# Layer norm, attention with rotary positions and a SwiGLU in one kernel: moments of two batches shared by tiles between two engines, two chunks of gate and up moved ahead, jobs reordered, first scores set between the last units of the prologue

## The reference

```python
xn = layernorm(x)                                  # no affine part
q, k, v = xn @ Wq.T + bq, xn @ Wk.T + bk, xn @ Wv.T + bv   # q: 16 heads of 8; k, v: 4 heads of 8
q, k = q * cos + rotate_half(q) * sin, k * cos + rotate_half(k) * sin
p = softmax(q k^T / sqrt(8))                       # over 1024 keys, per batch and head
attn = (p @ v) @ Wo.T + bo
ffn = (silu(xn @ wg.T) * (xn @ wu.T)) @ wd.T       # 384 hidden; int32 weights times 1/127
out = x + attn + ffn
```

## Time and profile before

| | |
|---|---|
| median of 3 runs | 758.31 us (757.91 to 759.13) |
| profiled execution | 758.32 us |
| span in the trace (first to last instruction) | 755.8 us |
| mean granted TensorE clock | 0.995 of full |
| busy: PE, DVE, ACT, POOL | 722.8, 683.1, 624.0, 228.7 us |
| first row maximum on DVE | 28.25 us |
| end of the prologue's weigh(0, 0, 0) | 65.82 us |

### The profile page before, as it was taken

One profiled execution on the slowest core, in us unless ns is written; L12 is line 12 of the kernel. 1 busy time (PEld: TensorE's weight loads), 2 busy tenths in 40 slices (PEclk: granted clock), 3 DMA queues, 4 the chain that ended last, 5 costly groups with the idle time before them and its releaser, 6 DMA issues.

```text
span 755.8 us, 13786 instructions
## 1 busy us (share of the span) xinstructions
PE 722.8 (96%) x4933; PEld 218.8 (29%) x4934; DVE 683.1 (90%) x1262; ACT 624.0 (83%) x1303; POOL 228.7 (30%) x373
## 2 busy tenths in 40 slices
PE   6899999999999999999999999999999999999987
PEld 5532222232222222232322222232322222232322
DVE  5898999999999999999999999999999999999931
ACT  4536988888898988889888888889888888989886
POOL 3676762235412762112021211211121221202100
PEclk9999999999999999999999999999999999999999
DMA  9334331011311112011111101011110101110020
GB/s 297 102 130 115 109 115 43 1 40 26 116 33 34 33 65 84 2 32 33 33 33 33 33 2 45 21 33 34 33 33 27 39 2 33 33 33 2 2 85 29
DMA packets 30723, 38.26 MB, mean 51 GB/s; under 512 B 5600, under 2 KB 20448, under 8 KB 30400
## 3 DMA queue, kind: packets, MB, share of 16 engines
q1 hardware_dynamic: 27680, 30.18, 14.0%
q0 software_dynamic: 1440, 4.72, 1.7%
q10 hardware_dynamic: 1536, 2.49, 1.0%
HBM read 23.28 MB, written 11.53 MB: 46 GB/s over the span
## 4 chain that ended last, share of the span: by engine, by line
PE 75%; DVE 14%; ACT 6%; DMA 2%; issue 2%; SPq 0%; POOL 0%; ACTq 0%; DVEq 0%; POOLq 0%
PE acc_ps L1184 29%; PE banks L1080 20%; DVE mx L925 13%; PE banks L1100 10%; PE banks L1104 7%; ACT probs L719 5%; PE banks L1191 4%; PE banks L1199 3%; DMA y_all<-in_x 2%; PE banks L1162 1%; PE banks L1040 1%; PE banks L1234 1%; PE banks L1207 1%; PE banks L1061 0%; DVE row_max L931 0%
## 5 line engine op out<-in xcount | busy, mean ns | idle before, releaser
L925 DVE TENSOR_REDUCE mx<-banks 128x1 f32<-128x512 f32 x1024 | 638.4, 682 | 30.0 <-PE banks L1080 26.7
L719 ACT ACTIVATE probs<-banks 128x512 f32<-128x512 f32 x1024 | 549.2, 606 | 93.3 <-PE banks L1100 88.1
L1100 PE MATMUL banks<-qc,kc 51*128 51x512 bf16 x1024 | 304.9, 383 | 11.2 <-ACT probs L719 6.1
L1080 PE MATMUL banks<-ka,qa 48*128 48x512 bf16 x1024 | 301.8, 382 | 7.4 <-DVE mx L925 7.4
L1184 PE MATMUL acc_ps<-probs,v_grp 128*32 128x512 f32 x2048 | 273.4, 606 | 1.2 <-ACT probs L719 1.0
L1080 PEld LDWEIGHTS banks<-ka,qa 48*128 48x128 bf16 x1024 | 67.1, 94 | 291.3 <-DVE mx L925 246.2
L578 POOL TENSOR_TENSOR neg_max<-row_max,nought 128x16 bf16<-128x16 f32 x32 | 7.1, 222 | 316.8 <-DVE row_max L931 309.5
L1100 PEld LDWEIGHTS banks<-qc,kc 51*128 51x128 bf16 x1024 | 64.3, 94 | 45.7 <-ACT probs L719 42.5
L1104 PE MATMUL banks<-xn_T,w_ffn 128*128 128x256 f32 x192 | 66.3, 429 | 0.0
L1184 PEld LDWEIGHTS acc_ps<-probs,v_grp 128*32 128x32 f32 x2048 | 40.3, 108 | 85.7 <-ACT probs L719 58.8
L602 POOL TENSOR_TENSOR gated<-gu 128x256 f32<-128x256 f32 x48 | 35.3, 735 | 73.7 <-ACT gu L801 73.7
(11 more groups left out here) (108 smaller groups left out, 354.5 us busy)
## 6 DMA issues: line engine op xcount, KB each, us to landing
qa<-q_rows SPq DMA_DIRECT2D x28, 192.0 KB, 3.4
qc<-q_rows SPq DMA_DIRECT2D x56, 96.0 KB, 2.7
q_rows<-part POOLq DMA_DIRECT2D x18, 256.0 KB, 4.1
ka<-k_later SPq DMA_DIRECT2D x24, 96.0 KB, 2.1
kc<-k_later SPq DMA_DIRECT2D x24, 96.0 KB, 2.2
out<-y_all SPq DMA_DIRECT2D x16, 128.0 KB, 2.0
y_all<-in_x SPq DMA_DIRECT2D x3, 512.0 KB, 11.9
k_rows<-part SPq DMA_DIRECT2D x6, 256.0 KB, 3.0
```

Source lines behind the costliest of these rows:

```text
L719: nc.scalar.activation(probs[:, s % SLOTS, j, :], banks[:, score_bank(g, G * s + j), :], ACT.Exp, scale=SCALE).then_inc(exp_done, 1)
L925: nc.vector.tensor_reduce(out=mx[:, h, col, k:k + 1], in_=ps, op=ALU.max, axis=AX.X).then_inc(max_done, 1)
L1080: nc.tensor.matmul(ps, qa[par][rows, j // 2, t * P:(t + 1) * P], ka[par][rows, k * W:(k + 1) * W], start=True, stop=True).then_inc(a_ready, 1)
L1100: nc.tensor.matmul(banks[:, score_bank(g, u), :], kc[par][rows, kt * P:(kt + 1) * P], qc[par][rows, h, j // 2, :], start=True, stop=True). ...
```

## The change

- **Moments.** ACT now makes sums and squares of tiles 0 to 3 (HT = 4) of batches 1 and 2; DVE takes tiles 4 to 7 of batches 1 and 2 and all of batch 3. DVE does its four tiles of batch 1 ahead of the first rotation, the others later. An epsilon step for ACT's sums (add_eps_sums) comes beside the one for DVE's tiles. The squares of batch 2 stand between the splits on ACT.
- **Low part.** Both halves' third parts are subtracted by DVE (low); POOL's subtraction goes.
- **FFN.** Parts 0 and 1 of group 0's gate and up are multiplied between the replications (after the third part of half 0, and after the first of half 1); part 2 follows unit 6. They use banks 0, acc_ps and 1, so the transposes of batch 1 use banks 2 and 3. keep_busy is left only ahead of half 0's replications.
- **Order of the jobs.** The query projection of batch 1 comes at units 8 and 10, values at 20 and 22, the last head at 24 to 30, the values' transposes at 32 and 34, queries of batches 2 and 3 at 36 to 42. ACT's copies and the numbers waited for follow (RAW_Q, RAW_LAST). The first maxima are transposed behind unit 37, not 36.
- **First scores.** The four scores of step 0 are issued behind units 44, 45, 46 and 47.

```diff
-PE_XN, PE_FFN, PE_S1, PE_V = (2, 4, 10, 12, 14, 16), (5, 7, 9), (18, 20, 22, 24), (26, 28)
-PE_VT, PE_Q = (33, 35), (30, 32, 37, 39, 41, 43)
-IDLE_X, IDLE_PARTS = 20, (3, 3, 0, 4, 2, 4)
-NEG_BEHIND = HU + 4
+PE_XN, PE_FFN, PE_Q1, PE_V = (2, 4, 12, 14, 16, 18), 6, (8, 10), (20, 22)
+PE_S1, PE_VT, PE_Q = (24, 26, 28, 30), (32, 34), (36, 38, 40, 42)
+IDLE_X, IDLE_PARTS = 20, (3, 3, 0)
...
-        xnt_banks = (banks[:, 0, :], acc_ps[:, :])
+        def xnt_bank(b, h):
+            return banks[:, 2 + h, :] if b == 1 else (banks[:, 0, :], acc_ps[:, :])[h]
...
-            return banks[:, (2, 3, 1)[c], :]
+            return (banks[:, 0, :], acc_ps[:, :], banks[:, 1, :])[c]
...
-            pool.wait_ge(part_res, 1)
-            pool.wait_ge(part_mid, 1)
-            nc.gpsimd.tensor_tensor(part[:, 0, 2, HALF[0]], res[:, HALF[0]], part[:, 0, 1, HALF[0]],
-                                    ALU.subtract).then_inc(part_lo[0], 1)
...
             root(slice(0, NT), 2 * NT + 1)
             sum_tiles(1)
+            sum_squares(1, range(HT))
             copy_xn_T(0)
-            sum_squares(1)
+            root_later(slice(NT, 2 * NT), 3 * NT + 2, 1)
+            sum_tiles(2)
             split_high(0)
+            sum_squares(2, range(HT // 2))
             split_mid(0)
-            root_later(slice(NT, 2 * NT), eps_done, 1)
+            sum_squares(2, range(HT // 2, HT))
+            split_high(1)
             copy_rows(0, ka[0][:, HALF[0]])
-            split_high(1)
             copy_rows(1, qa[0][:, 0, HALF[0]])
             split_mid(1)
             copy_rows(2, qa[0][:, 1, HALF[0]])
             copy_rows(3, ka[0][:, HALF[1]])
             for i in range(PAIRS):
                 copy_rows(4 + i, qa[0][:, i, HALF[1]])
-            root(slice(2 * NT, NTT), 6 * NT + 2)
+            root_later(slice(2 * NT, NTT), 6 * NT + 3, 2)
             copy_xn_T(1)
             nc.scalar.preload_act_table(ACT.Exp)
             for c in range(FC):
                 act.wait_ge(ffn_up, 2 * (c + 1))
                 nc.scalar.activation(th[:, c, :], first_ffn_bank(c)[:, 0:CH], ACT.Tanh, scale=0.5).then_inc(gu_done, 1)
                 nc.scalar.activation(gu[:, c, :], first_ffn_bank(c), ACT.Copy).then_inc(gu_done, 2)
+            act.wait_ge(const_in, 32)
+            copy_later(1, 0)
             for b in range(2, B):
                 copy_xn_T(b)
-            act.wait_ge(const_in, 32)
-            for n in range(2):
-                copy_later(0, n)
             act.wait_ge(vt_ps, 1)
             nc.scalar.activation(v_T[:, :], s_ps[:, 0, :, :], ACT.Identity,
                                  bias=bias_sb[:, B_V:B_V + 1]).then_inc(vt_done, 1)
-            copy_later(1, 1)
+            for n in range(2):
+                copy_later(0, n)
             act.wait_ge(v_ps, 1)
-            nc.scalar.activation(v_all[:, :, :, :], s_ps[:, 0, :, :], ACT.Copy).then_inc(v_done, 1)
+            nc.scalar.activation(v_all[:, :, :, :], s_ps[:, 1, :, :], ACT.Copy).then_inc(v_done, 1)
             copy_neg(0, 0, first_bank(NEG_BEHIND + 1))
-            copy_later(2, 1)
+            copy_later(2, 0)
             copy_later(3, 0)
             act.wait_ge(rope_sum, 2)
             exps(0, 0, range(G))
...
+            def add_eps_sums(b):
+                k = (b - 1) * HT
+                dve.wait_ge(sum_done, b * SUMS)
+                nc.vector.tensor_scalar(ve[:, b * NT:b * NT + HT], sums[:, 1, k:k + HT], 1.0 / D, EPS, ALU.mult,
+                                        ALU.add).then_inc(eps_done, 1)
...
-            token_stats(0)
-            aggregate(0, 0)
+            token_stats(range(NT))
+            aggregate(range(NT), NT)
             add_eps(slice(0, NT), 2 * NT)
             root(slice(0, NT), 0)
             dve.wait_ge(rstd_done, 1)
             normalise(dve, nc.vector, 0, xn_done, halves=2)
-            token_stats(2)
-            aggregate(2, 2 * NT + 1)
+            token_stats(range(NT + HT, 2 * NT))
+            aggregate(range(NT + HT, 2 * NT), 2 * NT + 1 + HT)
+            add_eps_sums(1)
+            add_eps(slice(NT + HT, 2 * NT), 3 * NT + 1)
             dve.wait_ge(const_in, 32)
             def rope_half(h):
@@ -897,6 +914,12 @@
                 dve.wait_ge(part_hi, h + 1)
                 nc.vector.tensor_tensor(res[:, HALF[h]], rot[:, HALF[h]], part[:, 0, 0, HALF[h]],
                                         ALU.subtract).then_inc(part_res, 1)
+            def low(h):
+                dve.wait_ge(part_res, h + 1)
+                dve.wait_ge(part_mid, h + 1)
+                nc.vector.tensor_tensor(part[:, 0, 2, HALF[h]], res[:, HALF[h]], part[:, 0, 1, HALF[h]],
+                                        ALU.subtract).then_inc(part_lo, 1)
             rotate(0, 0)
             rotate(0, 1)
@@ -904,19 +927,17 @@
             rotate(1, 0)
             rest_of_high(0)
             rotate(1, 1)
-            dve.wait_ge(sum_done, 2 * NT + 2)
-            nc.vector.tensor_scalar(ve[:, NT:2 * NT], sums[:, 1, :], 1.0 / D, EPS, ALU.mult, ALU.add)\
-                .then_inc(eps_done, 1)
+            low(0)
             rope_half(1)
             root(slice(NT, 2 * NT), 1)
             rest_of_high(1)
-            token_stats(3)
-            dve.wait_ge(part_res, 2)
-            dve.wait_ge(part_mid, 2)
-            nc.vector.tensor_tensor(part[:, 0, 2, HALF[1]], res[:, HALF[1]], part[:, 0, 1, HALF[1]],
-                                    ALU.subtract).then_inc(part_lo[1], 1)
-            aggregate(3, 4 * NT + 1)
-            add_eps(slice(2 * NT, NTT), 6 * NT + 1)
+            token_stats(range(2 * NT + HT, 3 * NT))
+            low(1)
+            aggregate(range(2 * NT + HT, 3 * NT), 3 * NT + 2 + HT)
+            token_stats(range(3 * NT, NTT))
+            aggregate(range(3 * NT, NTT), 5 * NT + 2)
+            add_eps_sums(2)
...
+                if b == 1:
+                    pe.wait_ge(select_done, 2 * (1 + PAIRS))
+                if b == 2:
+                    pe.wait_ge(gu_done, 3 * (h + 1))
...
             pe.wait_ge(select_in, 16)
             for h in range(2):
                 if h == 1:
                     pe.wait_ge(rope_mul, 2 * NH)
                 for n in range(PARTS):
-                    keep_busy(IDLE_PARTS[PARTS * h + n])
+                    if h == 0:
+                        keep_busy(IDLE_PARTS[n])
                     replicate(h, n)
+                    if h == 0 and n == PARTS - 1:
+                        pe.wait_ge(w_done, 1)
+                        first_ffn(0)
+                    if h == 1 and n == 0:
+                        first_ffn(1)
...
-                if a in PE_FFN:
-                    c = PE_FFN.index(a)
-                    if c == 0:
-                        pe.wait_ge(w_done, 1)
-                        pe.wait_ge(select_done, 2 * (1 + PAIRS))
-                    for n in range(2):
-                        ffn_in(0, n, c, first_ffn_bank(c)[:, n * CH:(n + 1) * CH])
-                if a in PE_S1:
-                    n, h = divmod(PE_S1.index(a), 2)
-                    if a == PE_S1[0]:
+                if a == PE_FFN:
+                    first_ffn(FC - 1)
+                if a in PE_Q1:
+                    h = PE_Q1.index(a)
+                    if h == 0:
                         pe.wait_ge(w_later_in, 16)
-                        pe.wait_ge(xnt_done, 2 * B)
-                        pe.wait_ge(gu_done, 3 * FC)
-                    c = C_S1 + 64 * n
-                    last = project_tiles(n, h, [c] + [c + 32] * (B - 1))
+                        pe.wait_ge(xnt_done, 4)
+                    last = project_q(1, 1, h)
                     if h == 1:
                         last.then_inc(q_ps, 1)
                 if a in PE_V:
                     h = PE_V.index(a)
                     if h == 0:
-                        pe.wait_ge(raw_done, 1)
+                        pe.wait_ge(xnt_done, 2 * B)
+                        pe.wait_ge(gu_done, 3 * FC)
                     last = project_tiles(0, h, [C_V] * B)
                     if h == 1:
                         last.then_inc(vt_ps, 1)
+                if a in PE_S1:
+                    n, h = divmod(PE_S1.index(a), 2)
+                    if h == 0 and n == 0:
+                        pe.wait_ge(raw_done, RAW_Q[1])
+                    if h == 0 and n == 1:
+                        pe.wait_ge(vt_done, 1)
+                    c = C_S1 + 64 * n
+                    last = project_tiles(1 - n, h, [c] + [c + 32] * (B - 1))
+                    if h == 1:
+                        last.then_inc(q_ps, 1)
                 if a in PE_VT:
                     h = PE_VT.index(a)
                     if h == 0:
                         pe.wait_ge(vt_done, 1)
+                        pe.wait_ge(raw_done, RAW_LAST[0])
                     for t in range(h * HT, (h + 1) * HT):
-                        last = nc.tensor.transpose(s_ps[:, 0, t // 4, t % 4 * P:(t % 4 + 1) * P],
```

(41 more changed lines are left out.)

71 lines of the change are left out of this document (42 added, 29 removed).

## The result

| | before | after |
|---|---|---|
| median | 758.1 us (5 runs, 757.81 to 759.13) | 754.24 us (5 runs, 752.47 to 754.51) |
| ratio of the times | | 0.994, 95% interval 0.9927 to 0.9953 |
| profiled execution, span | 758.32, 755.8 us | 752.47, 750.3 us |
| mean granted TensorE clock | 0.995 | 0.998 |

The change makes the kernel 3.9 us faster by the medians, 5.5 by the spans of the two profiled executions (5.85 with the time outside the span, 2.5 us before and 2.2 after). The after side has two levels: 752.47 and 752.52 us with a mean clock of 0.998, and 754.24 to 754.51 with 0.995 and 0.993. One stretch of 3.41 us at the lower clock (a low stretch) takes 0.0023 off the mean, half of 3.41 over 750.3, so these are runs with one low stretch (0.998) and runs with two or three.

What follows compares the result with a forecast made beforehand. TensorE was taken as the bound from unit 4 to 46, with VectorE's chain setting the start. Gains of 2.6 + 2.1 + 1.7 + 1.2 - 0.2 = 7.4 us gave 758.3 - 7.4 = 750.9, range 748.5 to 755.0.

Steps and rivals of the forecast that it cites:

- rival A: Clock falls between units 2 and 4, between last projection and weighing 0, or at both: 752.0 to 754.0 us, chance 0.27.
- Part 1: Start, up to the second maximum: shared moments let the first rotation start at 13.7 instead of 16.05; 2.6 us won.
- Part 2: The 48 units, TensorE taken as the bound: two of three chunks leave, 2 x 1.06 = 2.1 us won.
- Part 3: Last units: first scores behind units 44 to 47 end weighing 0 earlier, 1.7 us; step 1 at full clock, 1.2 more.
- B: Scores' waits hold up units 45 to 48 by as much as they save; only the start is won: 753.6, chance 0.13.
- D: Gain absorbed in the first groups by a release that the prologue does not move: 757.8, chance 0.04.
- C: Clock swings through the whole unit stage, slower from the fifth new low stretch: 759.8, chance 0.06.

Runs made afterwards that it cites:

- b_first_hole: The kernel before with ten more small products behind its projections and nothing else: 758.45 us against 758.71, ratio 0.9999.
- e_fill_both: The changed kernel with ten small TensorE products between units 2 and 4 and one behind each of the four first scores: 751.21 us, ratio to before 0.9896.
- e_fill_start: The changed kernel with ten small TensorE products between units 2 and 4, four behind unit 2 and six behind unit 3: 751.81 us against 753.7.
- h_low_pool: The changed kernel with fourteen small products (ten between units 2 and 4, four among first scores) and half 0's low part subtracted by GpSimd again: 750.72 us.
- e_scores_back: The changed kernel with its four first scores behind unit 47 again, all else as changed: 756.07 us.

## Why the prediction was right in its direction and off in its size

**The step that failed is the choice between the forecast and rival A.** I gave "the clock stays full" 0.50 and one or two falls 0.27. The fall at the first place came in both traces of the changed kernel, and none of its 11 runs reached full clock. What I had as evidence against was wrong: the 1.86 us of idling at 29.40 "did not cost the clock" in one trace, and b_first_hole shows that in another the same idling is followed by a fall. With the gaps filled the time is 751.2 (e_fill_both), 0.3 us from the 750.9 that was forecast, and part of that nearness is luck: its profiled run took 751.61, weighing 1 ended at 63.62 where the forecast has 62.5 (69.93 - 7.4), and 0.3 us less outside the span hid some of it. Rival A's 752.0 to 754.0 is where the lower runs are, and the median of 754.24 is just above it.

**The sum, term by term.** Between the two profiled executions the four terms measure 2.8, -0.1, 1.8 and 0.8, which is 5.3 us, where the forecast has 2.6, 2.1, 1.7 and 1.2 less 0.2, which is 7.4. What failed is part 2, and most of its miss is the low stretch. Two sums about rivals were also off: one fall at its low end is 750.9 + 0.6 = 751.5 and not 752.0, and five new falls give 750.9 + 8.5 = 759.4 and not 759.8.

**Part 1 (2.6 us).** Between the two profiled executions 2.8 (30.43 to 27.61). It was right for the pattern of landings that this trace had. In the other one the rotation gains nothing, which the forecast could not see from one trace and should have asked, since the whole term hung on one landing time. Of the additions beside GpSimd's scaling I took 0 and bounded 1.4: rows 15.37 and 16.88 have 0.75 and 1.04 us where 0.69 is usual, 0.4 together. How late an addition is depends on when GpSimd's instruction began. The second scaling began at 16.88 in this trace, with the addition:

```profile
16.88 1.16 POOL L520 TENSOR_SCALAR w_ffn<-wi_sb 128x384 f32<-128x384 int32 x1
```

An addition that starts 0.22 us behind the start of that scaling took 0.82 us (b_first_hole), one 0.26 behind it 0.78 (e_fill_start), one 0.37 behind it 0.69 (e_fill_both), and the row at 17.46 from which I took 0 started 0.70 behind it. So contention of the kind that the page GPSIMD Engine Reference of the Trainium skill names (section 8, Key points) is there after all, but in these traces only for additions that start with GpSimd's instruction or shortly behind it. The low part on VectorE gave nothing that can be measured (h_low_pool).

**Part 2 (2.1 us).** In the trace after, unit 47's maximum ends near 60.0 and not 58.0. From the start of the second maximum to that end it takes 32.4 us, 32.3 before and 30.9 at full clock (e_fill_both). So this execution won nothing in the unit stage. The low stretch took 1.5 us, 0.74 and 0.64 of it in the two slow products and the rest in units; and at full clock 1.4 is won and not 2.1. The missing 0.7 is VectorE's pace: in e_fill_both 31 maxima take 20.00 us with no idle time listed, 0.645 each, where the forecast's floor had 0.60 and called TensorE the bound. Undoing it costs 2.6 where the chunks stand in a row. At full clock the sign and the order of size were right.

**Part 3 (1.7 us, and 1.2 in step 1).** From unit 47's maximum to the end of weighing 0: 3.1 us before, 1.3 after, forecast 1.4. No score waited for the maxima. e_scores_back bears it out at equal clock (1.1 to 2.0). Step 1 took 3.30 us, 2.94 + 0.2 forecast. Here the clock stayed full in both traces of the changed kernel; that it can fall at this place is seen in e_fill_start, at 59.60.

**Rivals.** B is excluded by e_scores_back, D by the same 685.7 us behind weighing 1, and C by the changed kernel's ladder of times, which ends at three low stretches. TensorE: Matmul & The Clock Gate of the Trainium skill ("A second HAM failure mode: psum-queue depth-cycling") has the clock swing where TensorE idles briefly and often between groups of products. The traces agree in kind, with low stretches at 27.2, 30.1 and 59.6, though the idle times ahead of the one at 30.1 were long ones, 1.04 and 1.50 us; I had cited it and priced it too low.

## What to carry to other kernels

When a change shortens one engine's work ahead of a stage, look at what TensorE does in the hole that is left, and fill it with products that no one waits for; here that was worth 2.5 us beside the change's own 3.9. Look at all the holes together: one filled alone gave nothing, for the clock fell behind the next. Put such products only where TensorE truly waits: among scores behind unit 47, which ScalarE waits for, three pieces of 0.64 us stood in the chain of waits. A term that hangs on when one load lands wants two traces before it is counted.

## What the runs showed of the hardware that was not expected

- Filling one gap moved the low clock to the next one and left the time as it was (758.45 against 758.71 us).
- Run times of one kernel rise with the number of low stretches, readable from the mean granted clock: 756.6, 758.5 and 759.9 us at 0.998, 0.995 and 0.993 (medians of 16, 36 and 12 runs of the kernel before). One near the end of the span cost 0.6 us at most.
- The same list of loads lands in two patterns: 512 KB of batch 2 at 13.8 to 14.2 us or by 12.2, the other half of batch 1 by 8.3 or at 9.4 to 9.6.
- A product of 8 columns on VectorE took 0.89 us in place of 0.17 beside a two-input subtraction of GpSimd, in all five traces that have the subtraction, each time ending within 0.02 us of it.
- A VectorE addition of 128x512 that started together with GpSimd's scaling of 128x384 took 1.04 us, one that started 0.37 us behind it the usual 0.69.
